# Recall, scores and state update of a retention kernel on 64x64 quarters of TensorE, the state summed on VectorE

## The reference

```
q, k = rotary(x @ Wq), rotary(x @ Wk)      # 4 heads of 64
v    = x @ Wv                              # 4 heads of 128
step(S, (qb, kb, vb)):                     # one chunk after the other
    attn    = (qb @ kb.T) * D              # D: causal decay
    o_intra = attn @ vb
    o_inter = (qb * cross_q) @ S
    S_new   = gC * S + (kb * cross_k).T @ vb
out = rmsnorm(o) * silu(x @ Wg) @ Wo
x1  = layernorm(x + out);  x2 = layernorm(x1 + ffn(x1))
```

## Time and profile before

| what | value |
|---|---|
| median of three runs | 439.88 us |
| the profiled execution, its own time | 439.12 us |
| its span, first to last instruction | 437.3 us |
| PE busy | 424.6 us (97%) |
| DVE busy | 296.6 us (68%) |
| ACT busy | 265.8 us (61%) |
| POOL busy | 189.0 us (43%) |
| mean granted clock of TensorE | 0.997 of full speed |

### The profile page before, as it was taken

One profiled execution on the slowest core, in us unless ns is written; L12 is line 12 of the kernel. 1 busy time (PEld: TensorE's weight loads), 2 busy tenths in 40 slices (PEclk: granted clock), 3 DMA queues, 4 the chain that ended last, 5 costly groups with the idle time before them and its releaser, 6 DMA issues.

```text
span 437.3 us, 10954 instructions
## 1 busy us (share of the span) xinstructions
PE 424.6 (97%) x3600; PEld 393.6 (90%) x3600; DVE 296.6 (68%) x857; ACT 265.8 (61%) x819; POOL 189.0 (43%) x333
## 2 busy tenths in 40 slices
PE   7998999999999999999999999999999999999994
PEld 3786888999999999999999999999999999998983
DVE  4888565667766676656767666668666677766764
ACT  5567655476665675666565666566566666555541
POOL 2332233454443454434354444344543344443564
PEclk9999999999999999999999999999999999999998
DMA  7931010011110011110011111011110000100011
GB/s 236 364 144 51 0 49 1 27 37 37 37 30 18 28 38 38 37 36 12 25 35 36 36 36 36 0 36 36 36 36 13 29 9 15 37 13 13 14 37 39
DMA packets 16227, 19.59 MB, mean 45 GB/s; under 512 B 1472, under 2 KB 13760, under 8 KB 16192
## 3 DMA queue, kind: packets, MB, share of 16 engines
q1 hardware_dynamic: 16192, 19.14, 13.5%
HBM read 14.94 MB, written 4.19 MB: 44 GB/s over the span
## 4 chain that ended last, share of the span: by engine, by line
PE 92%; DVE 2%; POOL 1%; issue 1%; DMA 1%; ACT 1%; SPq 0%; POOLq 0%; DVEq 0%; ACTq 0%
PE b_rows L437 32%; PE b_ffn L437 19%; PE b_rows L455 9%; PE b_rows L451 6%; PE b_head L584 6%; PE b_head L555 4%; PE b_head L552 3%; PE b_state L598 3%; PE b_turn L613 3%; PE b_ffn L573 2%; PE b_turn L465 2%; DMA wf_int<-in_w_proj 1%; POOL h_lo L1488 1%; DVE wf_lo L1096 0%; POOL rs L1508 0%
## 5 line engine op out<-in xcount | busy, mean ns | idle before, releaser
L1488 POOL TENSOR_TENSOR h_lo<-wf_int,h_hi 128x256 fp32r<-128x256 f32 x96 | 71.1, 741 | 114.2 <-ACT h_hi L934 113.2
L437 PE MATMUL b_ffn<-x1T_hi,wf_hi 128*128 128x256 f32 x384 | 93.0, 279 | 0.0
L437 PE MATMUL b_ffn<-x1T_lo,wf_hi 128*128 128x256 f32 x384 | 92.4, 278 | 0.0
L437 PEld LDWEIGHTS b_ffn<-x1T_hi,wf_hi 128*128 128x128 f32 x384 | 72.2, 188 | 0.6 <-DVE wf_int L1228 0.2
L437 PEld LDWEIGHTS b_ffn<-x1T_lo,wf_hi 128*128 128x128 f32 x384 | 72.2, 188 | 0.4
L902 ACT ACTIVATE sq<-b_head 128x128 f32<-128x128 f32 x124 | 34.4, 277 | 54.7 <-PE b_head L584 51.7
L934 ACT CAST h_hi<-wf_int 128x256 fp32r<-128x256 f32 x96 | 39.3, 409 | 45.7 <-DVE wf_int L1228 45.1
L1506 POOL TENSOR_TENSOR ve<-mv,eps 128x1 f32<-128x1 f32 x64 | 14.2, 222 | 102.9 <-DVE mv L1316 95.4
L1307 DVE TENSOR_TENSOR z<-b_rows,x_sb 128x256 f32<-128x256 f32 x32 | 13.6, 424 | 56.3 <-PE b_rows L437 56.2
L1228 DVE TENSOR_TENSOR wf_int<-b_ffn,wf_int 128x256 f32<-128x256 f32 x96 | 40.1, 418 | 13.1 <-ACT wf_int L923 9.7
L923 ACT ACTIVATE wf_int<-b_ffn 128x256 f32<-128x256 f32 x96 | 37.3, 388 | 18.8 <-PE b_ffn L437 18.3
(11 more groups left out here) (146 smaller groups left out, 1190.3 us busy)
## 6 DMA issues: line engine op xcount, KB each, us to landing
xT_raw<-in_xT SPq DMA_DIRECT2D x16, 256.0 KB, 3.0
x_sb<-in_x SPq DMA_DIRECT2D x16, 256.0 KB, 2.8
out<-wf_int SPq DMA_DIRECT2D x32, 128.0 KB, 1.7
wf_int<-in_w_ffn SPq DMA_DIRECT2D x6, 384.0 KB, 7.3
wf_int<-in_w_proj SPq DMA_DIRECT2D x6, 256.0 KB, 4.9
rope_sb<-in_rope SPq DMA_DIRECT2D x4, 256.0 KB, 6.6
rope_q<-in_rope_by_row SPq DMA_DIRECT2D x2, 512.0 KB, 9.2
wo_raw<-in_w_o SPq DMA_DIRECT2D x1, 512.0 KB, 7.7
```

The lines of the kernel that those rows point to most:

```text
L437: mm = pe.matmul(dst, a, b, start=(i == 0 and j == 0 and not begun), stop=(i == n - 1 and j == len(passes) - 1 and not more), skip_group_c ...
L1488: pool.tensor_tensor(h_lo[:, ring, hb], h_full[:, u], h_hi[:, ring, hb].bitcast(F32), ALU.subtract).then_inc(h_split[j], 1)
```

## The change

From slot 8 on, three things are different.

- Recall and scores split each head's product into two halves of the output partitions (`half(i)`, `half(j)`), so that every product uses 64 rows and 64 columns of the array. The four heads' products become eight.
- The update of tiles 8 to 30 is split over the 128 tokens into two halves `j` of 64 rows: the half j=0 goes to `b_state`, the half j=1 to the right half of the feed-forward bank that the turned x1 goes to. Every tile starts its sums afresh. The ACT copy L910 is gone for these tiles; instead DVE adds both banks to `state` in SBUF with two operations (`add_state`), between `split_x1T` and `split_y`. Block j=0 of gate and up, which overwrites that bank, waits for `state_kept` in addition.
- The waits ahead of recall, scores and update move into `free_heads`, and are made ahead of the last matmul of the block j=2 of gate and up.

```
+        def update_bank(s, t, j):
+            return b_state[:, 0:2 * DV] if j == 0 else x1_bank(s, t)[:, 256:256 + 2 * DV]
...
+                        if last_waits and i == n - 1 and j == len(passes) - 1:
+                            last_waits()
...
+                                for i in range(2):
+                                    pe.matmul(o_of(n, h)[half(i)], q_of(n, tn, h)[:, half(i)], state[half(h), h // 2],
+                                              start=h < 2, stop=False, skip_group_check=True)
...
+                            for j in range(2):
+                                mm = pe.matmul(scores_of(n, h)[half(j)], qkT[half(h), 2 + h // 2, half(j)],
+                                               q_of(n, tn, h), start=(tn == 0 and h < 2), stop=True,
...
+                        for pr in range(2):
+                            for j in range(2):
+                                for h in (2 * pr, 2 * pr + 1):
+                                    mm = pe.matmul(update_bank(s, t, j)[half(h), pr * DV:(pr + 1) * DV],
+                                                   qk[half(j), tn % 2, 256 + h * DK:256 + (h + 1) * DK],
+                                                   v_sb[half(j), tn % 2, h * DV:(h + 1) * DV],
+                                                   start=pr == 0, stop=True, skip_group_check=True)
...
+                if j == 0 and not natural(s) and not (isinstance(s, int) and (s == NATURAL or s >= NT)) and t > 0:
+                    pe.wait_ge(state_kept, states_to(q, t - 1))
...
-                gate_up_block(s - 1, q1, t1, 2, wide)
+                gate_up_block(s - 1, q1, t1, 2, wide, None if natural(s) else lambda: free_heads(s, q, t))
...
-                if exists(s - 1) and tn < TS - 1:
+                if exists(s - 1) and natural(s - 1) and tn < TS - 1:
                     act.wait_ge(state_done, states_to(qn, tn))
                     act.copy(state[:], b_state[:, 0:2 * DV].rearrange("p (c n) -> p c n", c=2)).then_inc(state_kept, 1)
...
+            def add_state(s, q, t):
+                n, (qn, tn) = s - 1, back(q, t, 1)
+                if exists(n) and not natural(n) and tn < TS - 1:
+                    flat = state[:].rearrange("p c n -> p (c n)")
+                    dve.wait_ge(state_done, states_to(qn, tn))
+                    if tn == 0:
+                        dve.tensor_copy(flat, update_bank(s, t, 1)).then_inc(state_half, 1)
+                    else:
+                        dve.tensor_tensor(flat, update_bank(s, t, 1), flat, ALU.add).then_inc(state_half, 1)
+                    dve.wait_ge(state_half, states_to(qn, tn) - 6)
+                    dve.tensor_tensor(flat, update_bank(s, t, 0), flat, ALU.add).then_inc(state_kept, 1)
...
                 split_x1T(s, q, t)
+                add_state(s, q, t)
                 split_y(s, q, t)
```

More of the change, by code:

```diff
@@ L427, in _, with split_product @@
             turn_stages = [(2, yT_split), (0, qkT_kept)]
-            def split_product(dst, stat, mov, begun=False, more=False):
+            def split_product(dst, stat, mov, begun=False, more=False, last_waits=None):
                 n = len(stat)
@@ L530, in keys_and_queries, with free_heads @@
                     query_block(b_turn, 0, 0).then_inc(q_first_done, 1)
+            def free_heads(s, q, t):
+                n, (qn, tn) = s - 1, back(q, t, 1)
+                if not exists(n):
+                    return
+                pe.wait_ge(qkT_kept, n + 1)
+                if is_slot(n, 2):
+                    pe.wait_ge(y_ready, 1)
+                elif exists(n - 1) and not is_slot(n, 1):
+                    pe.wait_ge(masked, n)
+                    pe.wait_ge(y_ready, n)
+                if not natural(n):
+                    pe.wait_ge(q_rotated, s - 8 if tn % 2 else s - 7)
+                if tn > 0:
+                    pe.wait_ge(state_kept, states_to(qn, tn - 1))
+                elif exists(n - 2):
+                    pe.wait_ge(state_kept, states_to(qn, tn) - 1)
+                if tn < TS - 1:
+                    pe.wait_ge(v_copied, n + 1)
+                    if not natural(n):
+                        pe.wait_ge(h_ready[1], s - FFN_LAG)
             def recall_and_score(s, q, t):
@@ L589, in update_state @@
             def update_state(s, q, t):
-                n, (qn, tn) = s - 1, back(q, t, 1)
+                n, tn = s - 1, back(q, t, 1)[1]
                 if exists(n) and tn < TS - 1:
[L593 to L601, removed]
+                    if natural(n):
+                        for h in range(H):
+                            mm = pe.matmul(b_state[half(h), (h // 2) * DV:(h // 2 + 1) * DV],
+                                           qk[:, tn % 2, 256 + h * DK:256 + (h + 1) * DK],
+                                           v_sb[:, tn % 2, h * DV:(h + 1) * DV],
+                                           start=(tn == 0 and h < 2), stop=tn == TS - 2, skip_group_check=True)
+                    else:
+                        for pr in range(2):
[5 more added lines that the diff above has]
+                                                   start=pr == 0, stop=True, skip_group_check=True)
                     mm.then_inc(state_done, 1)
@@ L614, in turn_y, with gate_up_block @@
                     mm.then_inc(yT_done, 1)
-            def gate_up_block(s, q, t, j, wide):
+            def gate_up_block(s, q, t, j, wide, last_waits=None):
                 if not ffn_slot(s):
@@ L633, in gate_up_block @@
                             for k in range(KD)]
-                    mm = split_product(dst[:, kind * 256:(kind + 1) * 256], stat, mov)
+                    mm = split_product(dst[:, kind * 256:(kind + 1) * 256], stat, mov,
+                                       last_waits=last_waits if kind == 1 else None)
                 mm.then_inc(ffn_done[j], 1)
@@ L730, in drain @@
                 down(*at(-1), wide, free=(z1_ready, NT - 2))
-                gate_up_block(*at(-1), 2, wide)
+                gate_up_block(*at(-1), 2, wide, lambda: free_heads(*at(0)))
                 recall_and_score(*at(0))
```

27 lines of the change are left out of this document (13 added, 14 removed).

## The result

| | kernel before | changed kernel |
|---|---|---|
| median | 439.56 us (438.86 to 440.82, 12 runs) | 440.14 us (439.27 to 441.64, 12 runs) |
| the profiled execution | 439.12 us, span 437.3, clock 0.997 | 441.64 us, span 439.9, clock 0.998 |
| ratio of times, after to before | | 1.0018, 95% interval 1.0010 to 1.0026 |

The forecast was 439.9 us (437.1 to 442.8) and "within 0.3%". The time rose by 0.6 us between the medians and by 0.8 us by the ratio. The interval leaves out 1, so the changed kernel is slower by about 0.2%; that is no change by the forecast's bound of 0.3%. The question is what lies under it: several microseconds gained and as many lost.

What follows compares the result with a forecast made beforehand. PE, busy throughout the steady part, was taken as the bound. Terms -3.7 + 2.4 + 0.25 + 0.8 + 0.25 summed to 0.0 us, leaving 439.1 us profiled, 439.9 us against the median; range 437.1 to 442.8 us.

Steps and rivals of the forecast that it cites:

- The new group: PE's recall, scores and update on 64x64 quarters: one change of division goes, 0.20 us gained per slot, 0.05 without update.
- The change of division is the array's, not the wait's: Ahead of PE's groups: its 0.10 us belongs to the array, so hoisted waits gain nothing; otherwise 2.5 us more.
- The stall: PE's block j=0 load waits for DVE's two additions: 0.14 us in 17 slots, 2.4 us, plus 0.25 in unrolled ones.
- What I expected to see of it: In the waits list: PEld at L443 for DVE's state, 18 times, 0.10 to 0.20 us, one near 0.8 in slot 9.
- Slot 9: DVE, late there, sets the time: no gain counts, both additions delay PE's load by 0.8 us.
- The hoisted waits are for things done over 1 us before: Waits moved ahead of the last gate-and-up matmul are already met, so priced at nothing outside slot 32.
- The drain: Slot 32, the drain's first: the hoisted wait also holds back the last gate-and-up matmul, 0.25 us more.
- The two ways to be faster: PE's stall does not come, 437.1 us, or hoisted waits save 0.10 in each of 25 slots, 437.4 us; chance 0.24.
- The longer stall: PE's wait for DVE's second addition takes 0.30 us a slot, 2.9 us more, 442.8 us; chance 0.18.
- the 467 us: PE's groups: only two quarters run side by side, 0.44 us more for each of 62 groups, 27 us; chance 0.07.
- the 452 us of open loads: PE's groups: quarters sharing rows don't hide weight loads, 0.05 us in each of 248 rounds, 12 us; chance 0.03.

Runs made afterwards that it cites:

- sum_split: Changed kernel with DVE's addition from b_state moved ahead of the split of x1, the feed-forward bank's half staying behind it; 436.4 us, ratio 0.9930 to the kernel before.
- hoist_only: Kernel before with only the waits ahead of recall, scores and update hoisted to the last gate-and-up matmul; 440.06 us, ratio 1.0008 to the kernel before.
- sum_later: Changed kernel with one more 128x256 DVE operation ahead of the two additions; 446.45 us, ratio 1.0147 to the kernel before.
- drain_late: Changed kernel with slot 32's waits put back behind the last gate-and-up matmul, ahead of recall; 439.85 us, ratio 1.0008 to the kernel before.
- update_only: Kernel before with the update on 64x64 quarters, DVE's sum, added wait and hoisted waits, recall and scores unchanged; 445.47 us, ratio 1.0149.

## Why the prediction was right, point by point

- **The new group: right.** The forecast had 1.25 and 1.69 us from the last gate-and-up matmul to T, and 1.24 and 1.68 were measured; 1.25 for slots without update, measured 1.25. The gain per slot, freed from the stall in sum_split, is 0.20 to 0.21 and 0.05 to 0.06, as forecast; over the slots that is the 3.7 us of the sum. The 0.02 for the fourth tile's later start is there too: tiles start 7 ns apart in a round, and T comes 0.20 after the last of them.
- **The change of division is the array's, not the wait's: right.** The prediction took nothing for the hoisted waits and held 2.5 us open. hoist_only shows 0.21 without a wait, as before with one.
- **The stall: right.** Forecast: additions at T + 1.22 and T + 1.67, load at T + 2.14, 0.14 us. Measured: T + 1.22, T + 1.67, T + 2.15, 0.15 us. In unrolled slots the load is at T + 2.16 and the matmuls behind it are 0.17 late rather than 0.15, so 0.02 more there, where I had 0.05. Over 12 + 5 slots the stalls cost 2.65 us, as forecast. What I expected to see of it failed. I had written that the forecast is wrong if the wait is missing, and the list does not have it; the wait is there, but only the distance of the loads shows it, and sum_split and sum_later, which remove and lengthen it, bear it out.
- **Slot 9: right in sum, not in its parts.** The load is 0.80 later, as forecast. "The hoisted waits are for things done over 1 us before" failed here: the wait for `h_ready1` holds back the last gate-and-up matmul, and together with scores' later start this takes the slot's 0.20 us. The forecast priced all hoisted waits at nothing, and this one, which moved up because half of the update goes to the feed-forward bank, was among them. The forecast counted no gain in this slot, for another reason (DVE sets its time), and so the sum did not suffer.
- **The drain: right up to recall.** Forecast 0.25 (the parts, 0.11 + 0.21 - 0.05, make 0.27). The wait costs 0.50 - 0.22 = 0.28 us from y to recall, hoist_only and drain_late agree on it, and 0.05 come back with the first load. Behind slot 32 the forecast had nothing, and the profile has 0.59 us: slower steps and the transfer's landing.
- **What the sum lacked: slower steps.** My terms give 0.0 us, and the profile has 1.17 from slot 8 on. Trains of 256-column matmuls run at 0.118 us a step instead of 0.113 in places, and the change makes more of them. Counted over the whole program, the time above 0.113 is 3.22 us in the changed kernel, 2.31 in the one before and 2.36 in sum_split: 0.9 us. From slot 8 on, the four kernels with the stall have 2.8 to 3.2 us of it (changed, update_only, drain_late, sum_later) and the six without it 2.0 to 2.4. So the stall costs more than its own 0.15 us, though why PE steps slower behind it is not shown. Another 0.22 us of the 1.17 is the landing of the last transfer.
- **The rivals.** The two ways to be faster did not happen by themselves; the first is what sum_split makes on purpose, and its forecast of 437.1 us stands against 436.4. The longer stall did not come. Four quarters do run side by side: the 467 us were out of the question, as were the 452 us of open loads. The Trainium skill, "TensorE: Matmul & The Clock Gate" (Part 3, The mechanism), has a load overlap a running matmul only where the row group differs; the quarters of a pair share their rows, and their rounds keep 0.11 us all the same, so the trace goes against that rule for this shape; the same section also lets a load into the background weight buffer go ahead, and no run here can tell whether that is what happens. By its Part 1 (Wait — 56ns, not 53.3ns?), at about 62 ns for each matmul with hardware decode off, an estimate for 16 passes is 0.99 us. From the first start of scores to that of the update the trace has 0.44 us, so that limit did not bind.

The near zero was therefore not luck of one number: the gain and the stall were each within 0.02 us of what a slot showed. It was luck that the missing term stayed small: the slower steps, 0.9 us, are more than the forecast gave to slot 9, and only the bound of 0.3%, 1.3 us, took them in. And the zero is not a property of the quarters: with one DVE operation moved, sum_split is 3.7 us faster than the changed kernel.

## What to carry to other kernels

When work is put between an operation and the one that another engine waits for, take that engine's time of need from the trace and count forward from the last known start, operation by operation; a stall of 0.15 us is nothing, but it came 17 times. Where several results are summed out of different banks, take first what does not share the contended bank, in idle time that is already there. And before a wait is moved ahead of a further instruction, look at the slots where it is met late: the first slots of a new form and the drain. A result that moves to another bank brings that bank's own wait along, as `h_ready1` did here.

## What the runs showed of the hardware

- Four 64x64 fp32 tiles run together as freely as two larger ones: 16 passes in the time of 8 before (0.67 and 0.71 us), starts 7 ns apart in a round, rounds 0.11 us apart.
- A change of the array's division costs about 0.10 us over the ordinary step (0.21 and 0.11), with or without a wait at it (before and hoist_only), plus the first weight load, 0.10 us for 128 columns and 0.05 for 64.
- PE runs some trains of equal matmuls at a slower step, 0.118 instead of 0.113 us, with the granted clock shown as 1.00. Such a train behind the stall of T = 214.19 (12 steps from 217.27 to 218.68, 0.1175 each):

```profile
217.27 0.28 PE L443 MATMUL b_ffn<-x1T_lo,wf_hi 128*128 128x256 f32 x1
217.38 0.28 PE L443 MATMUL b_rows<-wo_hi,yT_hi 128*128 128x256 f32 x1
...
218.68 0.28 PE L443 MATMUL b_rows<-wo_hi,yT_lo 128*128 128x256 f32 x1
```

  Behind a pause some trains are 3 steps long, others 18, in the drain up to 58. But a pause is not needed: all ten profiles have a train of 7 steps in block j=2 of nearly every slot, behind matmuls without a gap (before: 210.07 to 210.89). What starts a train and what sets its length was not tested and stays open.
- The start-up of one execution took 1.4 us longer, with 0.63 us against 0.40 us for the same matmul and steps of 0.43 against 0.23 us, while the granted clock is shown as 1.00 for both. The factor of nearly two is all that the rows say of the cause. The last output transfer took from 1.70 us (hoist_only) to 3.10 us (update_only) to land. One profile by itself can so mislead about a change of this size; only distances from a common point inside the program (here T of slot 8) are compared.
